# The dense stages between three gather passes, written out chunk by chunk

## What is computed

```python
def sage_conv(x, W_l, b_l, W_r):
    agg = segment_sum(x[src], dst); cnt = number of edges that end in the node
    return (agg / maximum(cnt, 1)) @ W_l.T + b_l + x @ W_r.T
h   = relu(sage_conv(x, W1_l, b1_l, W1_r))
x   = layernorm(x + sage_conv(h, W2_l, b2_l, W2_r))
Q, K, V = x @ Wq.T + bq, x @ Wk.T + bk, x @ Wv.T + bv        # 4 heads of 16
Ee  = edge_attr @ We.T + be
s   = exp(clip((K[src] * Q[dst] / 4 * Ee).sum(over a head's 16), -5, 5))
out = layernorm(x + segment_sum(V[src] * s, dst))
```

## Time and profile before

| | us |
|---|---|
| median of the runs | 12097.26 |
| the profiled execution | 12102.03 |
| its span, first to last instruction | 12100.2 |
| busy: GpSimd (POOL) | 8855.2 (73%) |
| busy: TensorE matmuls / weight loads | 7526.1 (62%) / 7023.2 (58%) |
| busy: VectorE (DVE) | 3997.3 (33%) |
| busy: ScalarE (ACT) | 1891.3 (16%) |

### The profile page before, as it was taken

How to read it: one execution, slowest core, us unless ns; L and a number is a source line. 1 busy time by engine, 2 the same in 40 slices (tenths; PEclk the granted TensorE clock), 3 DMA queues, 4 the chain that set the end, 5 groups by cost and what they waited for, 6 DMA issues and landing times.

```text
span 12100.2 us, 168544 instructions
## 1 busy us (share of the span) xinstructions
PE 7526.1 (62%) x44520; PEld 7023.2 (58%) x44521; DVE 3997.3 (33%) x8639; ACT 1891.3 (16%) x4110; POOL 8855.2 (73%) x9383
## 2 busy tenths in 40 slices
PE   4555556666666555555555555676666677777776
PEld 4555555555555544445555555565666666677776
DVE  2222222222222211111222222244455555555555
ACT  1000000000000100000000000022223333333333
POOL 6777777777777577777777777727777777777775
PEclk6555555555556555555555555555555555555555
DMA  3222222222222122222222222212322333333332
GB/s 69 60 59 54 60 60 60 58 60 59 59 59 55 45 48 48 48 47 48 46 47 48 48 47 48 47 42 79 80 79 78 80 79 80 79 79 80 78 80 72
DMA packets 915624, 741.93 MB, mean 61 GB/s; under 512 B 509830, under 2 KB 765478, under 8 KB 915479
## 3 DMA queue, kind: packets, MB, share of 16 engines
q0 software_dynamic: 300000, 410.20, 15.3%
q1 hardware_dynamic: 534004, 229.11, 7.9%
q10 hardware_dynamic: 81600, 102.41, 2.4%
HBM read 625.83 MB, written 115.24 MB: 61 GB/s over the span
## 4 chain that ended last, share of the span: by engine, by line
POOL 68%; issue 24%; PE 4%; DMA 1%; DVE 1%; POOLq 1%; DVEq 1%; ACT 0%; SPq 0%; ACTq 0%
POOL kv L436 68%; PE ps_kv L462 1%; PE ps_q L520 1%; DMA kv<-in_x,src_ids 1%; PE ps_sum L462 1%; POOLq L433 0%; PE ps_q L462 0%; DMA kv<-h_rows,src_ids 0%; DVE hot L836 0%; PE ps_t L514 0%; PE ps_kv L535 0%; DMA kv<-kv_rows,src_ids 0%; POOLq L221 0%; ACT stageT L639 0%; PE ps_t L528 0%
## 5 line engine op out<-in xcount | busy, mean ns | idle before, releaser
L436 POOL DMA_INDIRECT kv<-kv_rows,src_ids x3125 | 2950.4, 944 | 1155.7 <-issue 948.4
L436 POOL DMA_INDIRECT kv<-h_rows,src_ids x3125 | 2953.1, 945 | 1046.4 <-issue 1038.5
L436 POOL DMA_INDIRECT kv<-in_x,src_ids x3125 | 2950.6, 944 | 978.7 <-issue 937.7
L462 PE MATMUL ps_q<-kv,hot 128*128 128x65 f32 x5000 | 1126.7, 406 | 1246.2 <-DMA kv<-h_rows,src_ids 650.0
L462 PEld LDWEIGHTS ps_q<-kv,hot 128*128 128x128 f32 x5000 | 1063.2, 317 | 1382.0 <-issue 1382.0
L836 DVE SCALAR_TENSOR_TENSOR hot<-dst_ids,base,ps_t 128x640 f32<-128x640 f32 (+2 forms) x1629 | 1434.1, 880 | 1028.5 <-issue 958.1
L462 PE MATMUL ps_sum<-kv,hot 128*128 128x65 f32 x5000 | 1068.5, 390 | 1115.0 <-DMA kv<-in_x,src_ids 478.2
L462 PEld LDWEIGHTS ps_sum<-kv,hot 128*128 128x128 f32 x5000 | 999.8, 300 | 1229.0 <-issue 1228.8
L462 PE MATMUL ps_kv<-kv,message 128*128 128x65 f32 x4440 | 1038.2, 417 | 970.4 <-DMA kv<-h_rows,src_ids 378.2
L462 PEld LDWEIGHTS ps_kv<-kv,message 128*128 128x128 f32 x4440 | 973.3, 327 | 1042.6 <-issue 1041.3
L565 PE MATMUL ps_sum<-message,node_h 128*128 128x64 f32 x6260 | 1466.4, 421 | 0.2 <-DVE message L984 0.2
(11 more groups left out here) (166 smaller groups left out, 6897.9 us busy)
## 6 DMA issues: line engine op xcount, KB each, us to landing
node_q<-in_edge_attr SPq DMA_DIRECT2D x125, 480.0 KB
edge_space<-ee_rows SPq DMA_DIRECT2D x125, 480.0 KB
kv<-in_x,src_ids POOLq DMA_INDIRECT x3125, 2.4
kv<-h_rows,src_ids POOLq DMA_INDIRECT x3125, 2.4
kv<-kv_rows,src_ids POOLq DMA_INDIRECT x3125
node_q<-in_edge_attr SPq DMA_DIRECT2D x125, 320.0 KB
edge_space<-ee_rows SPq DMA_DIRECT2D x125, 320.0 KB
ee_rows<-node_q ACTq DMA_DIRECT2D x25, 1440.0 KB, 5.7
```

What stands on the lines that cost most here:

```text
L436: nc.gpsimd.indirect_dma_start(out=into[:, u, k, 0:width], out_offset=None, in_=table_rows, in_offset=bass.IndirectOffsetOnAxis(ap=src_ids ...
L462: mm = nc.tensor.matmul(to[:, 0:D + 1], one_hots[:, k, :], kv[:, u, k, 0:D + 1], start=(k == 0), stop=(k == K - 1))
```

## The change

The table's three fields change places in the word (`before` in the low 16 bits, `first` next, `more` on top). All loops over chunks in stages A, B and C are written out as straight code. TensorE turns blocks straight out of `node_x` and `node_h`, so the ScalarE copies into `stage` are gone. A chunk is turned in two halves (4 and 3 blocks), each copied out by its own ScalarE copy.

- Stage A: turned blocks go to `ps_t` and `ps_kv` by turns, the copies to `stageT` and `stage` by turns, the products to `ps_q` and `ps_e` by turns. TensorE turns chunk c+1 before it multiplies chunk c.
- Stage B is one sequence: TensorE does multiply(c), turns the normed chunk c-1, turns the rows of c+1, and makes keys, values and queries of c-1. The halves rotate over three banks. Square and root run on ScalarE chunk by chunk, the scaling and the split of the queries (two copies, two subtractions) on GpSimd. Each of the four parts of a chunk's keys and values counts by itself.
- Stage C: the root, the reciprocal and the scaling (GpSimd) run chunk by chunk, and the stores follow each. A square root of one element is put ahead of stages B and C on ScalarE.
- One bank (`columns`), overwritten in B, is written again from `iota` before `att`.

```diff
+        kvq_parts = [(0, 2, ps_kv[:, 0:512]), (2, 2, ps_kv[:, 512:1024]), (4, 2, ps_e[:]), (6, 1, ps_hot32[:])]
+        one_banks = (halves_of((ps_t[:, 0:512], ps_t[:, 512:1024])), halves_of((ps_kv[:, 0:512], ps_kv[:, 512:1024])))
+        one_products = (ps_q, ps_e)
+        turned_rows = (stageT, stage)
+
+        two_banks = (ps_t[:, 0:512], ps_t[:, 512:1024], ps_sum[:])
+        two_order = []
+        for c in range(-1, CHUNKS + 1):
+            two_order += [("normed", c - 1, half) for half in range(2) if 0 <= c - 1]
+            two_order += [("rows", c + 1, half) for half in range(2) if c + 1 < CHUNKS]
...
+                pool.wait_ge(d.rooted, c + 1)
+                z = node_x[:, c * CH:(c + 1) * CH, D:2 * D]
+                nc.gpsimd.tensor_tensor(z, z, over_features(std[:, c * CH:(c + 1) * CH]), ALU.mult).then_inc(d.normed, 1)
+
+            def split_queries(c):
+                raw, rest = raw_queries[:, c % 2], raw_queries[:, 2]
+                into = node_q[:, c * CH:(c + 1) * CH, :]
+                pool.wait_ge(d_kvq.read, c + 1)
+                nc.gpsimd.tensor_copy(into[:, :, 0:D], raw).then_inc(d_kvq.step, 1)
+                pool.wait_ge(d_kvq.step, 3 * c + 1)
+                nc.gpsimd.tensor_tensor(rest, raw, into[:, :, 0:D], ALU.subtract).then_inc(d_kvq.step, 1)
+                pool.wait_ge(d_kvq.step, 3 * c + 2)
+                nc.gpsimd.tensor_copy(into[:, :, D:2 * D], rest).then_inc(d_kvq.step, 1)
+                pool.wait_ge(d_kvq.step, 3 * c + 3)
+                nc.gpsimd.tensor_tensor(into[:, :, 2 * D:], rest, into[:, :, D:2 * D], ALU.subtract).then_inc(d_kvq.split, 1)
+
+                pool.wait_ge(d_kvq.split, c + 1)
+            for c in range(CHUNKS):
+                scale(c, d_two)
+                if c > 0:
+                    split_queries(c - 1)
+            split_queries(CHUNKS - 1)
...
+            for c in range(CHUNKS):
+                scale(c, d_end)
...
+                def turn(c):
+                    pe.wait_ge(d.meant, c + 1)
+                    for half, (first, end, bank) in enumerate(one_banks[c % 2]):
+                        if c >= 2:
+
+                            pe.wait_ge(d.copied, 2 * (c - 2) + half + 1)
+                        turn_blocks(node_x, c, first, end, bank, d.turned)
+
+                def multiply(c):
+                    to = one_products[c % 2]
+                    pe.wait_ge(d.copied, 2 * c + 2)
+                    if c >= 2:
+                        pe.wait_ge(d.read, c - 1)
...
+                turn(0)
+                for c in range(CHUNKS):
+                    if c + 1 < CHUNKS:
+                        turn(c + 1)
+                    multiply(c)
...
+                    if kind == "rows":
+                        pe.wait_ge(d.meant, c + 1)
+                    else:
+                        pe.wait_ge(d.normed, c + 1)
+                    for half, (first, end) in enumerate(HALVES):
+                        at, bank = two_use(kind, c, half)
+                        if at >= 3:
+                            pe.wait_ge(d.copied, at - 2)
...
+                    pe.wait_ge(d.copied, two_use("rows", c, 1)[0] + 1)
+                    if c > 0:
+                        pe.wait_ge(d.read, c)
...
+                    pe.wait_ge(d.copied, two_use("normed", c, 1)[0] + 1)
+                    if c > 0:
+
+                        pe.wait_ge(kvq.read, c)
+                    else:
+                        pe.wait_ge(kvq.meant, 1)
...
+                turn("rows", 0)
+                for c in range(CHUNKS):
+                    multiply(c)
+                    if c > 0:
+                        turn("normed", c - 1)
+                    if c + 1 < CHUNKS:
+                        turn("rows", c + 1)
+                    if c > 0:
+                        keys_values_queries(c - 1)
+                turn("normed", CHUNKS - 1)
+                keys_values_queries(CHUNKS - 1)
...
+                for c in range(CHUNKS):
+                    for half, (first, end, bank) in enumerate(one_banks[c % 2]):
+                        act.wait_ge(d.turned, 2 * c + half + 1)
+                        copy_turned(bank, turned_rows[c % 2], first, end).then_inc(d.copied, 1)
...
+                stage_rows = stage
+                copy_part("rows", 0)
+                for c in range(CHUNKS):
+                    if c > 0:
+                        copy_part("normed", c - 1)
+                    if c + 1 < CHUNKS:
+                        copy_part("rows", c + 1)
+                    square(c, d, mid[:])
+                    root(c, d)
+                    if c > 0:
+                        keys_and_values(c - 1)
+                copy_part("normed", CHUNKS - 1)
+                keys_and_values(CHUNKS - 1)
...
+            nc.scalar.activation(unused[:], zero[:], ACT.Sqrt)
+            layer_two(d_two, d_kvq)
+            act.wait_ge(d_kvq.split, CHUNKS)
...
+            nc.scalar.activation(unused[:], zero[:], ACT.Sqrt)
+            for c in range(CHUNKS):
+                square(c, d_end, squares[:, c * CH:(c + 1) * CH, :])
+                if c > 0:
+                    root(c - 1, d_end)
+            root(CHUNKS - 1, d_end)
...
+                z = node_x[:, c * CH:(c + 1) * CH, D:2 * D]
+                v.tensor_reduce(total[:, c % 2], z, AX, ALU.add).then_inc(d.totalled, 1)
+                dve.wait_ge(d.totalled, c + 1)
+                v.scalar_tensor_tensor(z, over_features(total[:, c % 2]), -1.0 / D, z, ALU.mult, ALU.add).then_inc(d.centred, 1)
...
+                of = var[:, c * CH:(c + 1) * CH]
+                dve.wait_ge(d.squared, c + 1)
+                v.tensor_reduce(of, squared, AX, ALU.add).then_inc(d.spread, 1)
+                dve.wait_ge(d.spread, c + 1)
+                v.tensor_scalar(of, of, 1.0 / D, EPS, ALU.mult, ALU.add).then_inc(d.var, 1)
+
+            def inverse_root(c, d):
+                dve.wait_ge(d.std, c + 1)
+                of = std[:, c * CH:(c + 1) * CH]
+                v.reciprocal(of, of).then_inc(d.rooted, 1)
...
+            for c in range(CHUNKS):
+                mean(c, d_one, node_x)
+            for c in range(CHUNKS):
+                h = node_h[:, c * CH:(c + 1) * CH, D:2 * D]
                 dve.wait_ge(d_one.product, c + 1)
-                v.tensor_tensor(mid2[:], products, bias[:, 0:1, :].to_broadcast([P, CH, D]), ALU.add).then_inc(d_one.read, 1)
-                dve.wait_ge(d_one.read, c + 2)
-                h = node_h[:, bass.ds(c * CH, CH), D:2 * D]
-                v.tensor_scalar_max(h, mid2[:], 0.0).then_inc(d_one.ready, 1)
-
-                dve.wait_ge(d_one.ready, c + 1)
+                v.tensor_tensor(h, products_in(one_products[c % 2]), bias[:, 0:1, :].to_broadcast([P, CH, D]), ALU.add).then_inc(d_one.read, 1)
+                dve.wait_ge(d_one.read, c + 1)
+                v.tensor_scalar_max(h, h, 0.0).then_inc(d_one.ready, 1)
...
+            v.memset(stage[D:D + 1, :, :], 1.0).then_inc(d_kvq.meant, 1)
+
+            def queries(c):
+                if c >= 2:
+
+                    dve.wait_ge(d_kvq.split, c - 1)
+                for i, (first, count, part) in enumerate(kvq_parts):
+
+                    dve.wait_ge(d_kvq.ready, len(kvq_parts) * c + i + 1)
+                    read = v.tensor_scalar_mul(raw_queries[:, c % 2, first:first + count, :],
                 read.then_inc(d_kvq.read, 1)
+            mean(0, d_two, node_h)
+            mean(1, d_two, node_h)
+            for c in range(CHUNKS):
+                z = node_x[:, c * CH:(c + 1) * CH, D:2 * D]
+                dve.wait_ge(d_two.product, c + 1)
+                v.tensor_tensor(z, z, products_in(ps_q), ALU.add).then_inc(d_two.read, 1)
+                dve.wait_ge(d_two.read, c + 1)
+                centre(c, d_two)
+                if c + 2 < CHUNKS:
+                    mean(c + 2, d_two, node_h)
+                variance(c, d_two, mid[:])
+                inverse_root(c, d_two)
+                if c > 0:
+                    queries(c - 1)
+            queries(CHUNKS - 1)
+
+            st.link(v.tensor_copy(columns, iota[:]))
...
+            for c in range(CHUNKS):
+                centre(c, d_end)
+                if c > 0:
+                    variance(c - 1, d_end, squares[:, (c - 1) * CH:c * CH, :])
+                if c > 1:
+                    inverse_root(c - 2, d_end)
+            variance(CHUNKS - 1, d_end, squares[:, (CHUNKS - 1) * CH:, :])
+            inverse_root(CHUNKS - 2, d_end)
+            inverse_root(CHUNKS - 1, d_end)
```

More of the change, by code:

```diff
@@ L507, in sum_pairs, with turn_blocks @@
                             turn_attr(u, e, t * 16 + 16 * (phase * TURNS + 1))
[L509 to L518 removed]
+            def turn_blocks(nodes, c, first, end, bank, done, columns_of=slice(None)):
+                for i in range(first, end):
+                    tp = nc.tensor.transpose(bank[:, (i - first) * P:(i - first + 1) * P], nodes[:, c * CH + i, columns_of], ident[:])
+                tp.then_inc(done, 1)
```

(34 more changed lines are left out.)

185 lines of the change are left out of this document (61 added, 124 removed).

## The result

The kernel after takes 11936.15 us (median of 3, 11933.32 to 11936.7) against 12097.26: ratio 0.9866, 95% interval 0.9853 to 0.988. Its profiled execution has a span of 11931.5 us, 168.7 less than before's 12100.2.

The account below looks back on a forecast made before the run. The prediction took GpSimd's gathers to bound the passes and TensorE at the low clock to bound A and B. Savings of 14.8 + 34.3 + 9.7 = 58.8 us gave a median of 12038.5 us, range 12018 to 12065.

Parts of the forecast that it names:

- What bounds it: Three passes of some 3900 us: as long as GpSimd's gathers, 1.25 us apart; only stages A, B and C can move.
- rival 1: Stages A and B: without gaps TensorE's clock goes to 2.4 GHz, A 29 and B 57 us less, 11952 us; 6%.
- A's term: Stage A: the copy's 0.95 us and 14 TensorE waits of 0.99 us go; -14.8 us, bounds -8 to -18.
- the "fill" of the lower bound: Stage A: TensorE's pipeline fill at each switch, up to 0.2 us, might go too, in the bound of -18 us.
- B's term: Stage B: one sequence bound by TensorE's 11.09 us of work per chunk; -34.3 us, bounds -19 to -41.
- rivals 3 and 4: Stage B: unseen waits, 1.1 us more per chunk, 12054 (10%); GpSimd becomes the bound in B and C, 12170 (4%).
- C's term: Stage C: VectorE's period 2.65 us per chunk, scaling moved to GpSimd; -9.7 us, -13.9 without contention, -4.8 with 0.65.
- Rival 2: Stages B and C: ScalarE reloads tables between square and root, C saves nothing, total -49 us, 12048 us; 10%.
- The rest: Table word's fields and the passes: 0, 1 us either way; longer straight code: 0, up to 10 us as a bound.

Follow-up runs that it names:

- A's start parted: Kernel after, with TensorE waiting between turning chunk 0 and chunk 1 until VectorE has made all 13 chunks' means: stage A 74.8 us, B 110.7 us.
- B's order changed: Kernel after, with keys, values and queries in stage B placed between the two turnings, ScalarE's square moved to match: A 42.0 us, B 180.9 us.

## Why the prediction was wrong, point by point

**What bounds it** held: the gathers are 1.25 us apart as before, and all of the change is in A, B and C.

**The step that failed** is in rival 1, "TensorE's clock rises", put at 6%: "these are the same instructions", 6.34 us on end at 0.50. That the old loops stay at 0.50 said only that they don't raise the clock, not that they can't hold it: with the clock up at its start the old loop of A ran at 1.00 to its end. The new order puts two turnings on end, and behind such a pair the clock rose; the two kernels that take the pair away (A's start parted, B's order changed) have A and B at 0.50. That the pair is what raises it is argued from these two, which change other things as well, and two of six pairs in A didn't raise it; the cause of the rise stays open. In A the shares are measured: the order alone is worth 90.1 - 69.4 = 20.7 us at the low clock, the high clock alone 90.1 - 60.5 = 29.6 in the old loop, both 48.5. In B no run has the new order at the low clock throughout; by 10.35 us a chunk at 0.50 (A's start parted, before its rise) against 5.65 over the twelve chunks behind the rise, the clock is worth an estimated 12 x 4.7 = 56.4 of the 101.6 us and the order 45. With the order alone the three stages would be 20.7 + 45 + 12.6 = 78 us shorter, an estimated 12019 us, just inside the range; the clock took the time out of it.

**Rival 1's own sizes** came near: A 29 less than the forecast (27.8 between the two kinds of execution), B 57 less (56). B's is partly luck: it was 14 chunks going from 11.09 to some 7 us, and it is 12 going from 10.35 to 5.65.

**A's term** of -14.8: -20.7 at the low clock, beyond its bound of -18. The waits went as forecast. TensorE's period is 4.38 and not 4.75 us: a turning and the products behind it now overlap by 0.2 us too, and products that follow without a stop take 3.09 and not 3.25, the "fill" of the lower bound. No row of the kernel before showed the 0.2 us of that fill. 13 x 0.37 = 4.8 us of the 5.9 missed.

**B's term** of -34.3: -45 by the estimate above, beyond its bound of -41, for the same reason, 10.35 a chunk and not 11.09. GpSimd's five instructions take 0.94, 0.56, 1.03, up to 0.83 and up to 1.29 us, near the 1.0 taken; TensorE waited for the scale once, 1.3 us, so rivals 3 and 4 were nowhere near.

**C's term** of -9.7: -12.6. The period is 2.33 us, not 2.65. The centring is longer by 0.35 us per chunk where GpSimd scales beside it (0.3 taken, 0.65 for a full exclusion); the small instructions overlap the ends of the large ones. Of this gain the meeting of the engines at the end took 3.8 us back (4.0 for 0.2), which the prediction didn't have: it took the end from before.

**Rival 2**, tables: none. A single load stands ahead of B and one ahead of C. **The rest** was 0 as forecast: the passes with their last sums are 6.0 us shorter here, but in the long execution of the same kernel they are 8.2 us longer than here (11757.9), so this is scatter.

## What to carry over

Before counting TensorE's time at the clock that a trace shows, ask what would let it rise (a run of work on end that the new order creates) and, apart from that, whether the loop would hold it (here waits of 0.73 and 0.99 us in every chunk did no harm and single ones of 1.46 us and more did, with cases at the end of B between them); the first can be tried with a few dummy transposes before any loop is rewritten. A stage that got its clock from such a chance pair has two results, so time it often enough to see both. GpSimd, given a share of the last stage, cost 3.8 us at the program's end when it worked to the last store and nothing when it was done 10.6 us before; look at that wait when an engine is given work there.

## What the runs showed of the hardware

- A clock that was up stayed up through waits of TensorE of 0.73 and 0.99 us in every chunk, 14 times over; it fell in ten places behind a wait of 1.46 to 2.08 us. The size of one wait doesn't tell all: at the end of B it fell in seven traces behind waits of 0.7 and 1.3 us, one in each of two chunks.
- It rose in or right behind each of 8 bursts of 16 to 32 float32 transposes that began at 0.50, behind 4 of 6 of A's pairs of turnings (kernels with no burst there), and in none of 2 bursts of float32 products that began there (7.03 and 7.09 us on end). It rises in the mixed work of the passes as well. What exactly it takes is open.
- GpSimd: float32 `tensor_tensor` of 448 elements 0.94 us, a cast to bfloat16 0.56 or 0.83. VectorE's centring beside it 0.97 for 0.62 us.
- With GpSimd at work until the last stores, SyncE's wait at the program's end was 4.0 us in place of 0.2.
